# Five orders of issue in a pooled-attention kernel: U4 and refine, two low parts, cells, first queries, weight sums

## What is computed

```python
qk  = relu(bn(conv1x1(x, qk_w)))            # x: 8 x 512 x 64 x 64, qk: 256 channels
val = relu(bn(conv1x1(x, v_w)))             # 512 channels
key, value = psp(qk), psp(val).transpose(0, 2, 1)     # adaptive max pooling to 1, 3, 6, 8: 110 cells
query = qk.reshape(B, 256, 4096).transpose(0, 2, 1)
scores = softmax(einsum('bnc,bcs->bns', query, key) * 256 ** -0.5)
y = einsum('bns,bsc->bnc', scores, value)
return x + bn(conv1x1(y, out_w))            # fp32 throughout
```

## Time and profile before

| | us |
|---|---|
| median of 3 runs | 1330.21 |
| lowest, highest | 1327.58, 1331.76 |
| profiled execution, its own time | 1328.02 |
| span of the profile | 1326.2 |
| PE busy | 1284.6 (97%) |
| DVE busy | 957.4 (72%) |
| POOL busy | 952.3 (72%) |
| ACT busy | 688.2 (52%) |

### The profile page before, as it was taken

One profiled execution on the slowest core, in us unless ns is written; L12 is line 12 of the kernel. 1 busy time (PEld: TensorE's weight loads), 2 busy tenths in 40 slices (PEclk: granted clock), 3 DMA queues, 4 the chain that ended last, 5 costly groups with the idle time before them and its releaser, 6 DMA issues.

```text
span 1326.2 us, 16789 instructions
## 1 busy us (share of the span) xinstructions
PE 1284.6 (97%) x5539; PEld 1035.4 (78%) x5539; DVE 957.4 (72%) x2171; ACT 688.2 (52%) x1017; POOL 952.3 (72%) x414
## 2 busy tenths in 40 slices
PE   7999999999999999999999999999999998999996
PEld 6777788887888778887788877888788876888874
DVE  6455677778777778778777777777877776876566
ACT  4333555654555654455654455664455546654421
POOL 2888988876887867887777787887788734755622
PEclk9999999999999999999999999999999999999999
DMA  6323356666676646667556666656657668986226
GB/s 223 111 96 112 111 186 210 205 205 213 205 238 232 209 163 224 224 222 236 179 199 232 228 209 217 212 195 218 223 199 243 216 218 314 315 301 225 95 96 254
DMA packets 134537, 272.20 MB, mean 205 GB/s; under 512 B 9226, under 2 KB 9266, under 8 KB 134450
## 3 DMA queue, kind: packets, MB, share of 16 engines
q1 hardware_dynamic: 133874, 270.07, 60.3%
q10 hardware_dynamic: 576, 1.05, 0.2%
HBM read 174.61 MB, written 96.47 MB: 204 GB/s over the span
## 4 chain that ended last, share of the span: by engine, by line
PE 73%; DVE 10%; POOL 6%; ACT 6%; issue 3%; DMA 1%; SPq 0%; DVEq 0%; ACTq 0%; POOLq 0%
PE conv_ps L687 15%; PE conv_ps L689 15%; PE conv_ps L691 15%; POOL xl L578 5%; PE out_ps L773 3%; PE out_ps L774 3%; PE out_ps L775 3%; PE conv_ps L672 3%; PE conv_ps L673 3%; PE conv_ps L671 3%; DVE row_max L1319 2%; PE score_ps L744 2%; PE score_ps L745 2%; ACT xh L958 2%; PE score_ps L743 2%
## 5 line engine op out<-in xcount | busy, mean ns | idle before, releaser
L1319 DVE TENSOR_REDUCE row_max<-conv_ps 128x64 f32<-128x384 f32 (+2 forms) x576 | 283.7, 529 | 149.0 <-ACT q_out L1029 68.2
L578 POOL TENSOR_TENSOR xl<-xa,xh 128x1024 fp32r<-128x1024 f32 x108 | 257.7, 2409 | 87.0 <-ACT xh L958 87.0
L687 PE MATMUL conv_ps<-xh,sh 128*128 128x512 f32 x648 | 254.3, 392 | 8.8 <-DVE conv_ps L1382 3.1
L689 PE MATMUL conv_ps<-xh,sl 128*128 128x512 f32 x648 | 254.4, 393 | 0.0
L691 PE MATMUL conv_ps<-xl,sh 128*128 128x512 f32 x648 | 254.3, 392 | 0.0
L578 POOL TENSOR_TENSOR xl<-tt,xh 128x1024 fp32r<-128x1024 f32 x81 | 194.2, 2411 | 15.6 <-ACT xh L958 15.6
L687 PE MATMUL conv_ps<-xh,wh 128*128 128x512 f32 x486 | 189.5, 390 | 2.7 <-POOL xl L578 2.7
L691 PE MATMUL conv_ps<-xl,wh 128*128 128x512 f32 x486 | 190.8, 392 | 0.0
L689 PE MATMUL conv_ps<-xh,wl 128*128 128x512 f32 x486 | 190.7, 392 | 0.0
L966 ACT ACTIVATE conv_ps<-conv_ps 128x512 f32<-128x512 f32 x81 | 47.2, 583 | 260.4 <-PE conv_ps L691 249.5
L1459 DVE SCALAR_TENSOR_TENSOR xo<-out_ps,shift,xo 128x512 f32<-128x512 f32 x205 | 151.9, 745 | 30.5 <-PE out_ps L775 17.5
(11 more groups left out here) (227 smaller groups left out, 2537.5 us busy)
## 6 DMA issues: line engine op xcount, KB each, us to landing
xa<-x SPq DMA_DIRECT2D x148, 512.0 KB, 5.4
xo<-x SPq DMA_DIRECT2D x104, 512.0 KB, 4.2
out<-xo SPq DMA_DIRECT2D x104, 512.0 KB, 3.5
queries<-q_out SPq DMA_DIRECT2D x112, 256.0 KB, 2.3
q_in<-queries SPq DMA_DIRECT2D x50, 512.0 KB, 4.1
tt<-x SPq DMA_DIRECT2D x13, 512.0 KB, 5.2
out<-tt SPq DMA_DIRECT2D x13, 512.0 KB, 3.8
early<-queries SPq DMA_DIRECT2D x6, 512.0 KB, 7.1
```

Source lines behind the costliest of these rows:

```text
L578: nc.gpsimd.tensor_tensor(xl[:, b0:b1, :], raw, xh[:, b0:b1, :], ALU.subtract).then_inc(x_lo, 1)
L687: nc.tensor.matmul(out[:, :], hi[:, k, :], xh[:, b + k, :], start=first, stop=False, skip_group_check=True)
L689: nc.tensor.matmul(out[:, :], lo[:, k, :], xh[:, b + k, :], start=False, stop=False, skip_group_check=True)
L1319: last = nc.vector.tensor_reduce(row_max[:, c, n, :], src[:, r0_ * W:r1_ * W].rearrange("p (r w) -> p w r", w=W), AX.X, ALU.max)
```

## The change

Five steps are issued at another place; no instruction is added, removed or altered, and PE's, SP's and POOL's orders stay as they are.

1. In pairs in which a batch ended, DVE makes U4 of j = 0 ahead of the two instructions of `refine(B0)` instead of behind them.
2. In the same pairs DVE makes the low part of the values (`cell_values_lo`) ahead of the low part of the exponentials and U7 of j = 1 instead of behind them.
3. In the same pairs the cells of the second tile are pooled behind the last two row maxima of the pair instead of ahead of them.
4. In the first pair ACT splits part 4 of x behind the second query block of tile 1 and the copy of U1, instead of ahead of that query block.
5. In the first pair DVE makes the low part of the third weight sum (`combinations_lo(2)`) right behind that of the second one, ahead of U4, U7 and the row maxima of j = 1, instead of behind them.

```diff
--- before.py
+++ after.py
@@ -1109,7 +1109,6 @@
             for i in range(CC, PAR):
                 weights_hi(i)
             store_q(1, 0)
-            split_part_hi(1, 4)
             store_q(1, 1)
 
             for s in range(1, PAIRS):
@@ -1119,6 +1118,7 @@
                 batch_ended = A >= 0 and A % NT == 0
                 copy_u1(s, 0)
                 if s == 1:
+                    split_part_hi(1, 4)
                     split_part_hi(1, 5)
                 if B0 >= 0:
                     guess(B0)
@@ -1499,9 +1499,12 @@
                     pool_cells((t0 - 2) % NT, VC, CC, pair_group(s, 0))
                     pool_cells((t0 - 1) % NT, VC, CC, pair_group(s, 0))
                     finish_grids(VC, CC, keys_pooled)
+                if batch_ended:
+                    make_u4(s, 0)
                 if B0 >= 0:
                     refine(B0)
-                make_u4(s, 0)
+                if not batch_ended:
+                    make_u4(s, 0)
                 if B0 >= 0:
                     normalise(B0)
                 pool_pair_rows(s, 0, 0)
@@ -1517,6 +1520,7 @@
                 pool_pair_rows(s, 0, 3)
                 if s == 1:
                     combinations_lo(1)
+                    combinations_lo(2)
                 if B0 >= 0:
                     add_out(B0, 0)
                 if batch_ended:
@@ -1528,9 +1532,9 @@
                     if B0 >= 0:
                         add_out(B0, 2)
                     pool_pair_rows(s, 1, 0)
+                    cell_values_lo(A // NT)
                     split_e_lo(A)
                     make_u7(s, 1)
-                    cell_values_lo(A // NT)
                     pool_pair_rows(s, 1, 1)
                     pool_pair_rows(s, 1, 2)
                     if B0 >= 0:
@@ -1560,8 +1564,6 @@
                     if B0 >= 0:
                         add_out(B0, 2)
                     pool_pair_rows(s, 1, 3)
-                    if s == 1:
-                        combinations_lo(2)
                     if B0 >= 0:
                         add_out(B0, 3)
                     pool_cells(t0, 0, VC, pair_group(s, 2))
@@ -1580,9 +1582,10 @@
                     add_out(A, 0)
                 if batch_ended:
                     pool_cells(t0, 0, VC, pair_group(s, 2))
-                    pool_cells(t0 + 1, 0, VC, pair_group(s, 2))
                 pool_pair_rows(s, 2, 2)
                 pool_pair_rows(s, 2, 3)
+                if batch_ended:
+                    pool_cells(t0 + 1, 0, VC, pair_group(s, 2))
             for s in range(LAST, S):
                 ap, ac = s - NT - 1, s - NT
                 if s == LAST:
```

## The result

| | before | after |
|---|---|---|
| median of 6 runs, us | 1329.95 | 1322.43 |
| lowest, highest | 1327.58, 1334.95 | 1319.97, 1325.19 |
| ratio, 95% interval | | 0.9942 (0.992 to 0.9965) |
| profiled execution, span | 1328.02, 1326.2 | 1325.19, 1323.5 |
| PE, DVE busy | 1284.6, 957.4 | 1287.3, 949.4 |

By the ratio that is 7.7 us less, with an interval from 4.7 to 10.6 (the ratio's interval times 1330); by the two medians it is 7.5. The forecast was 9.2 less, 1321.0 us, and 1316.5 to 1326.5 for the range. The changed kernel was measured once more later: 1322.59 against 1329.73, ratio 0.9942 (0.9924 to 0.9961).

The account below looks back on a forecast made before the run. PE, busy 97% of the span, bounds the kernel, so only its waits can give time: 1.0 + 4.75 + 2.5 + 0 + 0.9 = 9.2 us off the median 1330.2 gives 1321.0, range 1316.5 to 1326.5.

Parts of the forecast that it names:

- Edit 1: U4 ahead of the refine: PE's 0.73 us wait goes, a new U7 wait leaves 0.2 a pair, 1.0 in five.
- U4's gain stays: Rival: PE meets no U7 wait, so 0.73 us a pair is kept instead of 0.2, 1318.3 in all; 15%.
- Edit 2: Values' low part earlier: PE's 0.71 us wait for add_out at project_values goes, 0.95 a pair in five, 4.75 us.
- s=4 had no such wait: In the first batch-end pair PE had no 0.71 us wait for add_out, so gain was counted in five pairs.
- slower rival: If POOL's last sum ends after 318.8, value_l loses the port and PE stands 3.4 us, five times: 1343; 3%.
- e_l and U7 don't move: At batch ends value_l's 0.62 us fits inside DVE's 1.31 us wait for e_h, so the steps behind keep their times.
- counting rule: A PE wait costs its idle time plus 0.24 us, since matmuls behind it start later than normal.
- locked out: The slower rival: value_l loses the DVE/POOL port for two POOL instructions, 4.8 us, in five pairs; 1343, 3%.
- Edit 3: Cells behind the last row maxima: ACT copies U1 earlier, PE saves 0.43 us in each of six pairs, 2.5 us.
- Edit 4: First pair's queries ahead of a split: PE's 1.4 us wait shrinks by 0.95, but POOL holds PE later: 0 us.
- Edit 5: Third weight sum earlier: PE's 1.66 us wait near 73.86 goes, but POOL's chain passes on only 0.9 us.
- The waits change places: Rival: PE meets another wait microseconds later; half of Edit 2 and Edit 3 and all Edit 1 lost, 1325.6; 22%.

Follow-up runs that it names:

- only_value: The kernel before with only the low part of the values moved ahead of that of the exponentials: 1326.47 us, ratio 0.997.
- only_cells: The kernel before with only the cells of the second tile moved behind the last row maxima: 1326.17 us, ratio 0.9976.
- only_queries: The kernel before with only the first pair's queries moved ahead of the split of part 4: run once, 1333.59 us.
- only_sums: The kernel before with only the low part of the third weight sum moved right behind the second: 1331.36 us, ratio 1.0003.
- after_no5: The changed kernel with the move of the third weight sum's low part undone: 1321.9 us, ratio 0.9928.
- after_again: The changed kernel, unaltered, measured once more on the same chip: 1322.59 us, ratio 0.9942.

## Why the prediction was right, step by step

**Edit 1: right.** Forecast 0.2 a pair kept of 0.73, with a new U7 wait of 0.37. Measured 0.15 alone, and U7's wait 0.39 in after. In the rows of DVE after, a step that doesn't need the one before starts 0.61 behind it, one that does 0.72 to 0.73. The Trainium skill ("VectorE: DVE Perf Modes", The DRAIN you can't avoid) says that a semaphore between two such steps costs nothing extra; by it 0.4 would have been kept, and the runs decide against it. "U4's gain stays" fell with it.

**Edit 2: right in four pairs of five, too high in sum.** 0.95 a pair was forecast and 0.9 to 1.0 measured in four of only_value's batches, 4.2 us in all instead of 4.75. Two steps failed. "s=4 had no such wait" was taken to mean that the edit is neutral there, though the pair runs the same code, and the slower rival's condition was set against POOL's times in s = 8 alone; in s = 4 POOL runs its sums without a pause from 156.81 on in before, and a value_l issued there meets one. In after this cost 0.57 + 0.24 = 0.8 by the counting rule and 0.7 in the stretch; in the five other executions with the early value_l it cost nothing, since U7 was in time. "e_l and U7 don't move" holds only if the `add_out` in front is on time: in s = 20 its x landed 2.69 us late, and the batch lost 0.6 to 0.7. DVE's waits for x doubled in sum between the two profiles:

```profile
DVE xo L1459 <- DMA xo<-x: 24.4, 21, 2.7
```

(before: 12.4 us in as many waits, 1.9 the longest). Edit 2 isn't shown to be the cause: only_cells, without it, has 22.3, and the 14 executions lie between 12.4 and 24.6. PE's rows of before could show nothing of this, since no wait of PE hung on it, but DVE's did, by the 1.87 in s = 20. Neither loss is in the forecast's sum; one of them is a rival's mechanism. The 3% for "locked out" was for five pairs with two POOL instructions lost in each. That never happened: in all 14 traces value_l took 2.85 us at most and ended when the POOL instruction under way was through.

**Edit 3: right.** 0.43 a pair forecast, 0.46 measured. ACT's copy of U1 started at 340.85, 0.32 behind PE's group, and not behind a row maximum:

```profile
340.85 0.58 ACT L966 ACTIVATE conv_ps<-conv_ps 128x512 f32<-128x512 f32 x1 [0.32 <-PE conv_ps L691]
```

**Edit 4: right**, nothing: POOL's chain took over the wait.

**Edit 5: right in its place, not shown in the time.** The first pairs, from PE's first product to the POOL wait in s = 4 (about 153), took 104.2 to 105.7 us in the eight executions with it (mean 104.8) and 105.4, 105.4, 106.0 and 106.3 in four without (mean 105.8; only_value and only_queries, 108.3 and 106.9, are left out: there the clock fell behind their waits of 2.82 and 1.98 for the third sum, which edit 5 does away with). That fits 0.9, but either group spreads over 0.9 to 1.5, and the ratio 1.0003 of only_sums and the pair after and after_no5 don't show a gain. The mean of kernels of different orders is weak evidence; it stays open whether any of it reaches the end.

**The waits change places: fell.** A batch took 156.4, not 157.5 or more, and beside the five waits for U7 of j = 0, which the forecast had counted, only the two named came, 0.4 and 0.6 us.

**The sum.** 9.2 was forecast. Measured were 7.4 in the stretch in which the edits act, 8.1 in the same stretch of after_again, and 7.7 by the ratio: within the range. In after most of what is missing is s = 4 (0.7), s = 20 (0.6) and a part of edit 5 (0.3). That after_again, without the loss in s = 4, has the same ratio shows that the times resolve no such terms; their account rests on the traces.

## What to carry to other kernels

An instruction moved ahead of one that PE waits for puts everything in front of it, its port and the loads before it, into PE's way: look at every pair that runs the code, the first too, and not only at the one whose trace you cost. In the trace of before, DVE's own waits for x already had their longest in s = 20, the pair that later held PE up. Where a wait goes, follow the engine's queue two steps further with its start-to-start times (0.60 without a dependence, 0.72 with one); here that gave the next wait to 0.02 us (0.37 forecast, 0.39 measured). Compare stages and medians; a span of one execution can hide a few us in its tail.

## What the runs showed of the hardware

- **The clock behind short waits.** In the first pairs some seven matmuls behind a wait of 2.82 us in only_value, and behind one of 1.98 in only_queries, start 0.43 apart, at the 1.2 GHz level (granted 0.89 from 70 to 85 us in both), but none do behind the 1.66 of before or the 2.60 of after_no5; behind the 4.4 us wait of the tail 8 matmuls ran so in before and 12 in after, and behind the one of 2.1 none in before and 14 in after. So the length of a wait alone doesn't tell what follows it. The times of the changed kernel's runs go with the mean granted clock of their spans: 1325.19 and 1324.22 at 0.993, 1321.93 to 1322.73 at 0.995, 1319.97 at 0.998.
- **The shared port by start, not by share.** value_l, a DVE subtraction with both inputs in SBUF, took 0.61 beside an idle POOL and up to 2.85 when a POOL instruction had begun just ahead of it. In all 52 places of the 14 traces where it began with more than 0.15 us of a POOL instruction to go, it ended 0.47 to 0.48 us behind that instruction's end, so it was never put off by a second one. The POOL instruction that followed within 0.1 us was drawn 2.66 to 2.80 long instead of 2.4; one that began 0.25 to 0.33 later was drawn 2.40 to 2.47.
- **Landing.** POOL's first sum in the pairs s = 2 to 4 began between 5.3 and 7.8 us behind the issue of its load. The two profiles of the changed kernel alone have 6.9, 7.8 and 7.6 against 7.0, 7.4 and 6.4.
